# Two conversions per hidden slice, from ScalarE to VectorE, in the feed-forward part of a transformer layer

## The reference, cut to what matters

```python
def float2fix(x, bits):            # round to multiples of 2^-bits
    s = 2.0 ** bits
    return round(x * s) / s

def pwlin_gelu_basic(x, ...):      # GELU, linear between 33 points 0.25 apart
    xq = float2fix(x, 8)
    y = interp(xq, PWL_X, PWL_Y)   # identity above 4, zero below -4
    return float2fix(y, 8)

def ffn(x, w1, b1, w2, b2):        # w1 1024x4096, w2 4096x1024
    h = float2fix(x @ w1 + b1, 8)
    h = float2fix(pwlin_gelu_basic(h), 8)
    return float2fix(h @ w2 + b2, 8)

x = x + attn(layernorm(x))         # one head, attention over channels; not touched
x = x + ffn(layernorm(x))
```

## Time and profile before

| | |
|---|---|
| time, median of 2 runs | 3643.53 us (3643.0 to 3644.06) |
| the profiled execution | 3642.69 us |
| its span, slowest core (core 6) | 3641.0 us; the 8 cores 3627.1 to 3641.0 us |
| mean granted TensorE clock | 0.795 to 0.798 of full speed on all cores |
| PE busy, of the span | 2132.8 us (59%) |
| VectorE (DVE) busy | 1283.3 us (35%) |
| ScalarE (ACT) busy | 993.1 us (27%) |
| GpSimd (POOL) busy | 29.0 us (1%) |

### The profile page before, as it was taken

The page is one execution under the profiler, slowest core; times in us unless marked ns, Lnnn a source line. Parts: engine busy times, 40 slices in busy tenths (PEclk is TensorE's granted clock), DMA queues, the critical chain, the costliest instruction groups (busy, mean ns, idle before and its releaser), DMA issues.

```text
span 3641.0 us, 26975 instructions; the slowest of 8 cores (3627.1 to 3641.0 us)
## 1 busy us (share of the span) xinstructions
PE 2132.8 (59%) x8086; PEld 822.1 (23%) x8086; DVE 1283.3 (35%) x2436; ACT 993.1 (27%) x1705; POOL 29.0 (1%) x106
## 2 busy tenths in 40 slices
PE   2020039777765967775376656666667566575674
PEld 2000013233322323321122212222222222221221
DVE  0000023221242322123362653635626456264462
ACT  0000410001230000122351552524515335153351
POOL 0000000000000000001000000000000000000000
PEclk9975569888887988787687877878778788787886
DMA  9979650100154010025402001010010100201101
GB/s 108 119 113 120 157 123 1 24 1 1 57 176 91 2 22 1 0 95 183 149 1 69 13 27 55 1 52 29 18 64 1 52 29 9 72 1 52 35 1 64
DMA packets 193562, 199.03 MB, mean 55 GB/s; under 512 B 156422, under 2 KB 156550, under 8 KB 191370
## 3 DMA queue, kind: packets, MB, share of 16 engines
q1 hardware_dynamic: 170540, 105.03, 11.6%
q0 software_dynamic: 4448, 50.33, 9.7%
q10 hardware_dynamic: 18432, 41.95, 3.1%
HBM read 151.14 MB, written 75.50 MB: 62 GB/s over the span
## 4 chain that ended last, share of the span: by engine, by line
PE 38%; ACT 17%; DVE 14%; DMA 10%; issue 8%; another core or an unknown queue 7%; SPq 3%; ACTq 1%; POOL 1%; DVEq 1%; POOLq 0%
PE pf L802 8%; PE pf L922 6%; PE pf L485 6%; DMA ys<-fX 5%; PE pf L627 4%; ACT yt L873 4%; PE pf L520 4%; PE pf L569 3%; DMA xst<-xs 3%; ACT hs0f L845 2%; ACT hs1f L845 2%; PE pf L886 2%; SPq L264 2%; DVE hs0f L853 2%
## 5 line engine op out<-in xcount | busy, mean ns | idle before, releaser
L802 PE MATMUL pf<-z2cm,w1b 128*128 128x512 bf16 x2048 | 624.8, 462 | 509.6 <-ACT hs0i L814 251.7
L802 PEld LDWEIGHTS pf<-z2cm,w1b 128*128 128x128 bf16 x2048 | 210.6, 110 | 896.5 <-issue 769.0
L886 PE MATMUL pf<-w2b,yt 128*128 128x512 bf16 x1024 | 327.6, 452 | 110.8 <-ACT yt L873 110.8
L922 PE MATMUL pf<-w2b,yt 128*128 128x512 bf16 x1024 | 248.6, 404 | 113.8 <-DVE fY1I L947 113.8
L485 PE MATMUL pf<-W1q,xcm 128*128 128x512 bf16 x1024 | 236.8, 385 | 45.7 <-DVE xcm L466 45.7
L814 ACT ACTIVATE hs0i<-pf,st_b1adj 128x512 int32<-128x512 f32 x128 | 85.5, 668 | 533.6 <-DVE fX L952 475.0
L947 DVE CAST fY1I<-pf 128x512 int32<-128x512 f32 x64 | 44.3, 692 | 449.6 <-PE pf L931 267.6
L886 PEld LDWEIGHTS pf<-w2b,yt 128*128 128x128 bf16 x1024 | 115.7, 115 | 307.4 <-issue 240.3
L441 PE MATMUL pf<-identf,strm 128*2 128x128 f32 x64 | 18.7, 395 | 277.6 <-DVE strm L416 244.0
L666 PE MATMUL pf<-pwT,acm 128*128 128x512 bf16 x512 | 146.2, 437 | 57.7 <-DVE x1t L692 55.0
L586 ACT ACT_TABLE_LOAD x2 | 2.6, 1283 | 625.3 <-DVE mbc L578 625.3
(11 more groups left out here) (127 smaller groups left out, 2346.6 us busy)
## 6 DMA issues: line engine op xcount, KB each, us to landing
xst<-xs SPq DMA_DIRECT2D x64, 512.0 KB, 3.7
x1b<-x1scr SPq DMA_DIRECT2D x64, 512.0 KB, 3.8
x1scr<-x1t ACTq DMA_DIRECT2D x32, 512.0 KB, 3.6
ys<-fX ACTq DMA_DIRECT2D x64, 256.0 KB, 3.5
x16scr<-xs POOLq DMA_DIRECT2D x2, 4096.0 KB, 63.0
w116scr<-w POOLq DMA_DIRECT2D x1, 8192.0 KB, 83.7
w216scr<-w POOLq DMA_DIRECT2D x1, 8192.0 KB, 160.3
z2scr<-z2t ACTq DMA_DIRECT2D x32, 256.0 KB, 2.1
```

The source lines that it names most:

```text
L802: t.matmul(pf[:, off:off + 512], w1b[:, j, 128 * ft:128 * (ft + 1)], z2cm[:, j, :], start=(j == 0), stop=(j == ND - 1)))
L886: t.matmul(pf[:, off2:off2 + 512], yt[:, ftw, 128 * tt:128 * (tt + 1)], w2b[:, ftw, 0:512], start=(ftw == 0), stop=False))
L922: t.matmul(pf[:, off:off + 512], yt[:, ft, 128 * tt:128 * (tt + 1)], w2b[:, ft, 512:1024], start=(ft == 0), stop=False))
```

## The change

The two conversions of `emit_act2` become two VectorE instructions at the end of `emit_tail`: a `tensor_copy` from float32 to int32, and a `tensor_scalar` that multiplies the int32 by 1.0 and writes bf16 to `yt`. `emit_act2` and its call are gone. Each new instruction waits for the one ahead of it through VectorE's own semaphore. The matmuls that read `yt`, and the next users of the chain's tiles, now wait for VectorE's count and not for ScalarE's. The rounding and what is computed stay as they were.

```diff
@@ emit_tail
                                lambda v_, Fv=Fv: v_.scalar_tensor_tensor(out=Fv[0][:], in0=Fv[4][:], scalar=256.0,
                                                                          in1=Fv[2][:], op0=ALU.mult, op1=ALU.add))
-                    t3v[ft] = dve3
-
-                def emit_act2(ft):
-                    S_ = HS[ft % 2]
-                    Fv, Iv = S_["f"], S_["i"]
-                    wait("scalar", "cDV", t3v[ft])
-                    vy1 = inc("scalar", "cAC", 1,
-                              lambda sc, Iv=Iv, Fv=Fv: sc.activation(out=Iv[1][:], in_=Fv[0][:],
-                                                                     func=AF.Identity))
-                    wait("scalar", "cAC", vy1)
-                    wait_drain("scalar", ("ytr", ft))
-                    q = inc("scalar", "cAC", 1,
-                            lambda sc, ft=ft, Iv=Iv: sc.activation(out=yt[:, ft, :], in_=Iv[1][:],
-                                                                   func=AF.Identity))
-                    fill[("yt", ft)] = q
-                    drain[("chain", ft % 2)] = [("cAC", q)]
+                    wait("vector", "cDV", dve3)
+                    dvy1 = inc("vector", "cDV", 1,
+                               lambda v_, Iv=Iv, Fv=Fv: v_.tensor_copy(out=Iv[1][:], in_=Fv[0][:]))
+                    wait("vector", "cDV", dvy1)
+                    wait_drain("vector", ("ytr", ft))
+                    dvq = inc("vector", "cDV", 1,
+                              lambda v_, ft=ft, Iv=Iv: v_.tensor_scalar(out=yt[:, ft, :], in0=Iv[1][:],
+                                                                        scalar1=1.0, scalar2=None, op0=ALU.mult))
+                    fill[("yt", ft)] = dvq
+                    drain[("chain", ft % 2)] = [("cDV", dvq)]
@@ w2_sl0_partial
-                    wait("tensor", "cAC", fill[("yt", ftw)])
+                    wait("tensor", "cDV", fill[("yt", ftw)])
@@ the loop over ft
-                    if ft >= 1:
-                        emit_act2(ft - 1)
@@ the second 512 columns (L922)
-                            wait("tensor", "cAC", fill[("yt", ft)])
+                            wait("tensor", "cDV", fill[("yt", ft)])
```

## The result

The changed kernel takes 3923.15 us (median of 12 runs) beside 3645.35 us for the kernel before (10 runs): 1.0757 times as long, 95% interval 1.0745 to 1.0769. The profiled execution of the changed kernel took 3920.34 us, with a span of 3918.4 us on its slowest core; before it was 3642.69 and 3641.0. In both series some executions had one die, or both, at a lower granted clock and took 2.3 to 3.4% longer; ratios here are made without them, so the first is not quite the quotient of the two medians.

What follows compares the result with a forecast made beforehand. It took a VectorE-ScalarE circle of 5.05 us a turn to bound the loop, not one engine's load. From 3642.7 us, +267.8 for 248 longer turns and -3.4 at chunk ends gave 3907 us, range 3888 to 3940.

Steps and rivals of the forecast that it cites:

- Two tied paths of 5.05 us, and nothing gained on ScalarE: Hidden-slice loop: from L859 to the next L842, ScalarE's and VectorE's paths both take 2.11 us; shortening ScalarE's alone brings 0.
- the circle: Feed-forward loop: VectorE and ScalarE hand each slice round, L859 to L859 in 5.05 us; PE is not in it.
- The durations, 0.43 from L833 as the nearest row: Each new VectorE instruction takes 0.43 us, bounds 0.40 and 0.48, as L833 matches input, output and width most nearly.
- full-rate rival: One or both new VectorE instructions take 0.69 us like L947: 3972 us with one, 4036 with both; chance 0.08.
- The starts 0.80, 0.54, 0.35: L859 to copy, copy to multiply, multiply to L826: 1.69 us instead of 0.61, 1.08 more a turn, +267.8 us.
- rival of cheap waits: On VectorE the pair costs two starts without a wait, 0.35 us each, 0.70 a turn: 3813 us; chance 0.04.
- The new waits counted at 0: PE's waits on VectorE's count, and those of the tiles' next users, delay nothing further: 0 us.
- The end of a chunk, 1.91 from L859 to PE: After a chunk's last slice, L859 to PE's L886 falls from 2.33 to 1.91 us, 8 times: -3.4 us.
- The gap does not take the pair in: VectorE's 1.44 us idle ahead of L853 cannot absorb the pair, as its list runs in order; rival 3639 us, chance 0.02.
- The clock: Rival: the lower clock level holds through L922's 128 matmuls behind the loop, 25 us a chunk, 4107 us; chance 0.02.
- ScalarE 323 us less: Profile after: ScalarE busy about 323 us less, from 256 slices at 1.26 us each.
- Irregular turns kept: Loop turns with some tenths more, 0.7 us a chunk, stay in the sum; those caused by PE would go, at most 6 us.

## Why the prediction was right, point by point

It gave 3907 us, 3888 to 3940, slower. The median is 3923.15, the profiled execution 3920.34, 13 us above the forecast. Of these 13 us, 10 lie in the loops (277.9 for 267.8), and 3 in what the slowest core happened to have outside them: 5.8 more ahead of the first L859, less 2.9 at the chunk ends beyond the 3.4 forecast. That the time still lies in the range is in part luck: its upper part was there for durations of up to 0.48, which did not come, and not for the wait that did.

- *Two tied paths of 5.05 us, and nothing gained on ScalarE*: shown for VectorE's path and for the nothing gained; ScalarE's length rests on rows 3 alone. With ScalarE's path 0.78 shorter the turn stayed at 5.05, and with the pair out of the circle it stayed at 5.05 with ScalarE relieved.
- *The durations, 0.43 from L833 as the nearest row*: the copy takes 427 ns and the multiply 426 to 427. The full-rate rival (3972 to 4036) is out; L947's 692 ns belongs to its PSUM input or to something else that the conversion itself does not bring.
- *The starts 0.80, 0.54, 0.35*: measured 0.79 to 0.80, 0.53 and 0.34 in the first chunk. There the turn is 6.11 against 6.13 forecast. The rival of cheap waits (3813) is out. The rule from which it came, that the semaphore costs nothing extra (the Trainium skill, VectorE: DVE Perf Modes, "The DRAIN you can't avoid"), does not describe these kernels, though they agree with the same section's remark that an instruction which is not held starts earlier: with a wait on the instruction ahead VectorE started 0.79 to 0.80 behind L859, without one 0.61, and taking such neighbours apart was part of what brought the loop to 2.93.
- *The new waits counted at 0*: this is the term that was mis-sized. The sentence on the next users of the tiles dealt with who is delayed, and not with the wait instruction itself. The one for `yt`, written behind the wait for the copy, costs 0.07 us in 7 chunks: 0.07 x 31 x 7 = 15 us. With it gone the loops took 15.4 us less, and the ratio fell from 1.0757 to 1.0707, 0.5% or 18 us. The turn that is 0.02 shorter than summed gives back 5 us.
- *The end of a chunk, 1.91 from L859 to PE*: 2512.75 - 2510.78 = 1.97, with the same 0.07 in it.

```profile
2512.75 1.87 PE L880 MATMUL pf<-w2b,yt 128*128 128x512 bf16 x4 [4.31 <-DVE yt L867]
```

- *The gap does not take the pair in* (rival, 3639 us): right for the order as written, and the experiment with the pair behind L833 shows what it said would be needed: 0.9983.
- *The clock*: the 128 matmuls of the second 512 columns, eight times, are busy for 248.3 us in all, 248.6 before. The rival is out.
- *ScalarE 323 us less*: 305. The 323 summed durations; in the busy time L873 and the L842 behind it overlapped.
- *Irregular turns kept*: 0.72 to 1.40 us a chunk after, 0.70 to 1.21 before. They did not go when the turn grew longer, as I had thought of those that PE might cause. A VectorE instruction starts about 0.35 late now and then, in every kernel with the old order, also behind one that it waits for on its own engine (seven times behind L856 before); why stays open.

## What to carry to other kernels

Where two engines hand a tile back and forth, follow the starts once round the circle before moving work: add up each path between the two points where they meet. In these kernels an instruction cost nothing in a gap longer than itself, and its full start-to-start with its wait on the circle, whatever the engines' busy shares said, and the first question about a circle is whether a different order of the lists can take it apart. Write the wait that comes last, last: satisfied waits ahead of it were free on VectorE here, behind it they were 0.07 us each.

## What the runs showed of the hardware that I had not expected

- A satisfied wait on VectorE costs 0.07 us behind the wait that releases the instruction (6.11, 6.18, 6.31 us a turn with none, one and three), and nothing ahead of it (6.11 with three).
- VectorE converts float32 to int32 and int32 to bf16 within SBUF, 128x512, in 427 ns, where the same conversions took 632 and 630 ns on ScalarE, and float32 to int32 out of PSUM takes 692 ns on VectorE.
- VectorE held a loop of 99% busy time (90.36 of 90.99 us) with six instructions a turn and waits on ScalarE's semaphore and on its own, each starting 0.08 to 0.09 us before the end of the one ahead (0.60 us behind one of 0.69, 0.40 behind one of 0.48).
